# New job orders for all five engines, and two pairs of tensors at another byte offset

## The reference

```python
x = x + _layernorm(_L0_attn_ref(_layernorm(x, axis=-1), w_qkv, b_qkv, w_out, b_out), axis=-1)
x = x + _layernorm(_L0_ffn_ref(_layernorm(x, axis=-1), W1, b1, W2, b2), axis=-1)
```

## Time and profile before

| | |
|---|---|
| median of 3 runs | 2037.46 us (2028.71 to 2041.54) |
| the profiled execution | 2037.54 us, of which the span from first to last instruction is 2035.8 us |
| granted TensorE clock, mean over the span | 0.979 |
| busy: PE, DVE, ACT, POOL | 1906.9, 1496.3, 1416.3, 744.5 us |

### The profile page before, as it was taken

One profiled execution on the slowest core, in us unless ns is written; L12 is line 12 of the kernel. 1 busy time (PEld: TensorE's weight loads), 2 busy tenths in 40 slices (PEclk: granted clock), 3 DMA queues, 4 the chain that ended last, 5 costly groups with the idle time before them and its releaser, 6 DMA issues. The chain is left out here.

```text
span 2035.8 us, 69000 instructions
## 1 busy us (share of the span) xinstructions
PE 1906.9 (94%) x26496; PEld 1547.0 (76%) x26496; DVE 1496.3 (74%) x2690; ACT 1416.3 (70%) x2375; POOL 744.5 (37%) x910
## 2 busy tenths in 40 slices
PE   6779999999999999999999999999999999999975
PEld 5558877778877777878777787777788777777765
DVE  4587887777777877787787778777777887786631
ACT  1556777777767867777777777677777777776653
POOL 2123334344323434333343433333443334333343
PEclk8889999999999999999999999999999999999998
DMA  5454554545545445555544455454455555444320
GB/s 139 94 113 118 121 120 107 125 109 125 121 115 127 107 116 116 121 122 121 124 110 116 116 121 123 120 128 102 114 122 120 122 121 127 107 115 102 81 65 16
DMA packets 203973, 229.65 MB, mean 113 GB/s; under 512 B 67808, under 2 KB 120800, under 8 KB 203744
## 3 DMA queue, kind: packets, MB, share of 16 engines
q1 hardware_dynamic: 201712, 223.36, 46.5%
q10 hardware_dynamic: 2032, 2.69, 0.4%
HBM read 71.77 MB, written 52.43 MB: 61 GB/s over the span
## 5 line engine op out<-in xcount | busy, mean ns | idle before, releaser
L894 DVE TENSOR_REDUCE max_bias<-p_pair 128x4 f32<-128x1024 f32 (+1 forms) x640 | 767.2, 1219 | 293.8 <-PE p_pair L635 171.4
L812 ACT ACTIVATE probs<-p_pair 128x1024 f32<-128x1024 f32 x640 | 642.9, 1031 | 295.5 <-PE p_pair L635 221.8
L1037 POOL TENSOR_TENSOR h_lo<-h_f,h_hi 128x512 fp32r<-128x512 f32 x256 | 338.7, 1324 | 589.7 <-ACT h_hi L849 582.1
L638 PE MATMUL p_pair<-stacks 49*128 49x256 f32 (+1 forms) x3072 | 294.8, 297 | 51.3 <-DVE max_bias L894 20.0
L638 PEld LDWEIGHTS p_pair<-stacks 49*128 49x128 f32 (+1 forms) x3072 | 225.7, 187 | 128.8 <-DVE max_bias L894 40.9
L665 PE MATMUL p_pair<-x_hi,w_hi 64*128 64x256 f32 (+1 forms) x2560 | 303.9, 313 | 4.2 <-DVE x_lo L908 3.8
L665 PE MATMUL p_pair<-w_hi,h_hi 64*128 64x256 f32 x2048 | 291.2, 280 | 12.4 <-POOL h_lo L1037 12.1
L665 PE MATMUL p_pair<-w_lo,h_hi 64*128 64x256 f32 x2048 | 288.7, 277 | 0.0
L665 PE MATMUL p_pair<-w_hi,h_lo 64*128 64x256 f32 x2048 | 288.5, 277 | 0.0
L665 PE MATMUL p_pair<-x_lo,w_hi 64*128 64x256 f32 (+1 forms) x2560 | 287.7, 300 | 0.0
L665 PE MATMUL p_pair<-x_hi,w_lo 64*128 64x256 f32 (+1 forms) x2560 | 287.4, 300 | 0.0
(11 more groups left out here) (80 smaller groups left out, 2706.5 us busy)
## 6 DMA issues: line engine op xcount, KB each, us to landing
stacks<-qk SPq DMA_DIRECT2D x1536, 64.0 KB, 2.3
o_rows<-o_t SPq DMA_DIRECT2D x128, 256.0 KB, 2.2
xr<-x SPq DMA_DIRECT2D x32, 512.0 KB, 6.0
inv_b<-inv_rows SPq DMA_DIRECT2D x64, 256.0 KB, 3.4
ya<-o_rows SPq DMA_DIRECT2D x64, 256.0 KB, 3.5
out<-yf SPq DMA_DIRECT2D x64, 256.0 KB, 2.3
xa<-x SPq DMA_DIRECT2D x31, 512.0 KB, 4.2
shift_rows<-max_t SPq DMA_DIRECT2D x128, 8.0 KB, 2.7
```

Of the source, the lines that this page charges most:

```text
L638: last = nc.tensor.matmul(dst[:, j, col:col + HALF].rearrange("p (a n) -> p a n", a=2), stack[r, stationary, at, kb * P:(kb + 1) * P], two ...
L812: nc.scalar.activation(probs[:, prob_slot(quad, c), :, :], banks("scores", n)[:, :, :], ACT.Exp, scale=SCALE).then_inc(exp_done, 1)
L894: nc.vector.tensor_reduce(dst, src, axis=AX.X, op=ALU.max, negate=True).then_inc(red_done, 1)
L1037: nc.gpsimd.tensor_tensor(h_parts[1][:, m:m + 2, :], h_f[:, n % 2, :, :], h_parts[0][:, m:m + 2, :].bitcast(F32), ALU.subtract).then_inc(h ...
```

## The change

All lists in `ORDER`, `FIRST` and `LAST` are new; the jobs are the same, 70 on PE, 64 on DVE, 46 on ACT, 20 on POOL and 30 on SP in a turn, each once, with some batch offsets and PSUM pairs changed. `FIRST` and `LAST` hold the same work but for where the turns are cut (PE 173 jobs ahead of the loop before, 171 after). No job's instructions change. In SBUF, the four `bn` tensors (96 bytes each, 384 together) move from behind `zeros` to ahead of `o2_t`. So `o2_*`, `h_hi`, `h_lo`, `max_bias`, `max_t`, `values` and the constants start 384 bytes higher, which takes the first five from 64 to 192 modulo 256; `xr` and `x2_*` move by whole multiples of 256. The diff, cut to PE's turn, two lines of DVE's, the start of PE's `FIRST` and the layout:

```diff
 ORDER = {
     "PE": [
-        ("f1", 7, -4, 3), ("scores_max", 1, -1, 2), ("qk", 3, -1, 1), ("scores_max", 2, -1, 0),
-        ("pv", 1, -2, 2), ("scores", 12, -2, 1), ("scores_max", 3, -1, 3), ("f2", 2, -4, 0),
-        ("scores", 13, -2, 2), ("scores_max", 4, -1, 1), ("scores", 14, -2, 3), ("f2", 3, -4, 0),
-        ("max_t", 0, -1, 2), ("scores", 15, -2, 1), ("scores", 16, -2, 3), ("scores_max", 5, -1, 0),
-        ("pv", 2, -2, 2), ("scores_max", 6, -1, 3), ("scores", 17, -2, 0), ("scores_max", 7, -1, 2),
-        ("scores", 18, -2, 1), ("scores_max", 8, -1, 3), ("scores", 19, -2, 0), ("scores_max", 9, -1, 1),
-        ("v", 0, -1, 2), ("scores_max", 10, -1, 3), ("pv", 3, -2, 0), ("x2", 0, -3, 1), ("scores", 0, -1, 3),
-        ("max_t", 1, -1, 0), ("v", 1, -1, 2), ("scores", 1, -1, 0), ("scores", 2, -1, 3), ("f1", 0, -3, 1),
-        ("scores_max", 11, -1, 0), ("x1", 0, 0, 3), ("f1", 2, -3, 2), ("scores", 3, -1, 0), ("f1", 1, -3, 1),
-        ("scores_max", 12, -1, 3), ("qk", 0, 0, 0), ("scores_max", 13, -1, 3), ("f1", 3, -3, 2),
-        ("qk", 1, 0, 0), ("scores_max", 14, -1, 3), ("op", 0, -2, 1), ("max_t", 2, -1, 3), ("op", 1, -2, 1),
-        ("scores", 4, -1, 2), ("f2", 0, -3, 0), ("scores_max", 15, -1, 3), ("scores_max", 16, -1, 2),
-        ("scores", 5, -1, 1), ("f2", 1, -3, 0), ("scores_max", 17, -1, 3), ("scores", 6, -1, 1),
-        ("pv", 0, -1, 2), ("scores", 7, -1, 0), ("scores_max", 18, -1, 1), ("scores", 8, -1, 3),
-        ("f1", 4, -3, 2), ("scores_max", 19, -1, 0), ("scores", 9, -1, 1), ("f1", 6, -3, 3),
-        ("scores", 10, -1, 0), ("scores_max", 0, 0, 1), ("f1", 5, -3, 2), ("max_t", 3, -1, 0), ("qk", 2, 0, 1),
-        ("scores", 11, -1, 0),
+        ("f1", 7, -4, 3), ("scores", 11, -2, 0), ("qk", 2, -1, 1), ("scores_max", 1, -1, 2), ("qk", 3, -1, 1),
+        ("scores_max", 2, -1, 0), ("pv", 1, -2, 2), ("scores_max", 3, -1, 0), ("scores", 12, -2, 1),
+        ("scores_max", 4, -1, 2), ("f2", 2, -4, 3), ("max_t", 0, -1, 0), ("scores", 13, -2, 2),
+        ("scores_max", 5, -1, 1), ("scores", 14, -2, 0), ("f2", 3, -4, 3), ("scores", 15, -2, 2),
+        ("scores_max", 6, -1, 1), ("scores", 16, -2, 0), ("pv", 2, -2, 3), ("scores", 17, -2, 0),
+        ("scores_max", 7, -1, 2), ("scores", 18, -2, 1), ("scores", 19, -2, 3), ("scores_max", 8, -1, 0),
+        ("v", 0, -1, 2), ("scores_max", 9, -1, 1), ("scores", 0, -1, 3), ("pv", 3, -2, 0), ("scores", 1, -1, 1),
+        ("scores_max", 10, -1, 3), ("x2", 0, -3, 0), ("scores", 2, -1, 1), ("v", 1, -1, 2), ("x1", 0, 0, 3),
+        ("max_t", 1, -1, 0), ("f1", 0, -3, 1), ("f1", 2, -3, 2), ("scores_max", 11, -1, 3),
+        ("scores", 3, -1, 0), ("f1", 1, -3, 1), ("scores_max", 12, -1, 3), ("qk", 0, 0, 0),
+        ("scores_max", 13, -1, 3), ("f1", 3, -3, 2), ("scores", 4, -1, 1), ("qk", 1, 0, 0),
+        ("scores_max", 14, -1, 3), ("op", 0, -2, 1), ("max_t", 2, -1, 3), ("op", 1, -2, 1),
+        ("scores", 5, -1, 0), ("f2", 0, -3, 3), ("scores_max", 15, -1, 2), ("scores_max", 16, -1, 1),
+        ("f2", 1, -3, 3), ("scores", 6, -1, 0), ("pv", 0, -1, 2), ("scores", 7, -1, 0),
+        ("scores_max", 17, -1, 1), ("scores", 8, -1, 3), ("f1", 4, -3, 2), ("scores", 9, -1, 0),
+        ("scores_max", 18, -1, 1), ("f1", 6, -3, 3), ("scores", 10, -1, 0), ("scores_max", 19, -1, 1),
+        ("f1", 5, -3, 2), ("scores_max", 0, 0, 0), ("max_t", 3, -1, 1),
     ],
...
     "DVE": [
...
-        ("copy_max", 2, -2), ("qk_lo", 1, -1), ("op_out", 0, -3), ("reduce", 15, -2), ("reduce", 16, -2),
-        ("lny_stats", 0, -3), ("lny_stats", 1, -3), ("f2_out", 0, -4), ("reduce", 17, -2), ("lnf_stats", 0, -4),
...
+        ("op_out", 0, -3), ("reduce", 15, -2), ("f2_out", 0, -4), ("lny_stats", 0, -3), ("reduce", 16, -2),
+        ("lny_stats", 1, -3), ("reduce", 17, -2), ("ln1_mean", 0, 0), ("lny_mean", 0, -3), ("reduce", 18, -2),
...
 FIRST = {
     "PE": [
-        ("x1", 0, 0), ("qk", 0, 0), ("qk", 1, 0), ("scores_max", 0, 0), ("qk", 2, 0), ("scores_max", 1, 0),
-        ("scores_max", 2, 0), ("scores_max", 3, 0), ("qk", 3, 0), ("scores_max", 4, 0), ("scores_max", 5, 0),
-        ("max_t", 0, 0), ("scores_max", 6, 0), ("scores_max", 7, 0), ("scores_max", 8, 0), ("scores_max", 9, 0),
...
+        ("x1", 0, 0), ("qk", 0, 0), ("qk", 1, 0), ("qk", 2, 0), ("qk", 3, 0), ("scores_max", 0, 0),
+        ("scores_max", 1, 0), ("scores_max", 2, 0), ("scores_max", 3, 0), ("scores_max", 4, 0), ("max_t", 0, 0),
+        ("scores_max", 5, 0), ("scores_max", 6, 0), ("scores_max", 7, 0), ("scores_max", 8, 0), ("v", 0, 0),
...
@@ -387,9 +406,11 @@
         xa = sb("xa", [P, KB, D])
         x1_t = [sb(f"x1_{n}", [P, KD, L], F32R) for n in ("hi", "lo")]
         o_t = sb("o_t", [P, 2, L])
-        o2_t = [sb(f"o2_{n}", [P, KD, L], F32R) for n in ("hi", "lo")]
         xr = sb("xr", [P, KB, D])
         x2_t = [sb(f"x2_{n}", [P, KD, L], F32R) for n in ("hi", "lo")]
+        KINDS = ("ln1", "lny", "ln2", "lnf")
+        bn = {n: sb(f"bn_{n}", [P, KB, 6]) for n in KINDS}
+        o2_t = [sb(f"o2_{n}", [P, KD, L], F32R) for n in ("hi", "lo")]
         h_parts = [sb(f"h_{n}", [P, KF, HALF], F32R) for n in ("hi", "lo")]
 
         max_bias = sb("max_bias", [P, 2, 8 * KB + D])
@@ -400,8 +421,6 @@
         values = sb("values", [P, KB, H * VW + 32 - VW])
         minus_half, eps = sb("minus_half", [P, KB]), sb("eps", [P, KB])
         zeros = sb("zeros", [P, P])
-        KINDS = ("ln1", "lny", "ln2", "lnf")
-        bn = {n: sb(f"bn_{n}", [P, KB, 6]) for n in KINDS}
         mv = {n: sb(f"mv_{n}", [P, KB, 2]) for n in KINDS}
         ve = {n: sb(f"ve_{n}", [P, KB]) for n in KINDS}
         rstd = {n: sb(f"rstd_{n}", [P, KB]) for n in KINDS}
```

438 lines of the change are left out of this document (225 added, 213 removed), and 17 rows, old and new, of tables (FIRST, LAST).

## The result

The changed kernel takes 2051.36 us (median of 6, 2048.24 to 2052.92), where the kernel before took 2039.5 (2028.71 to 2046.52) beside it: ratio 1.0066, interval 1.0048 to 1.0085. It is slower by 0.7%; the forecast was 2009 us and its range ended at 2038. The profiled execution took 2052.92 us.

What follows compares the result with a forecast made beforehand. PE, busy 94% of the span, was taken to bound the kernel through matmul pitch, short waits and ramps. Orders 11, layout 13 and start 5 us sum to 29, so 2037.5 becomes 2008.5, say 2009 us; range 1997 to 2018, 8-in-10 1993 to 2038.

Steps and rivals of the forecast that it cites:

- The orders in a turn: Steady-state loop: new orders leave PE's PSUM pair openers 2.38 us short instead of 2.86; taken as 0.4 us a turn, 11 us.
- POOL's list: POOL's new order in the turn: priced at nothing, since POOL is 37% busy and the other distances have room.
- The list of openers: PE's jobs in a turn that come too soon for their pair's reader: seven before, eight after the change.
- R3: Rival, DVE's queue blocks at f2_out 0 ahead of reduce 16: slower, 2050 us at 1 us a turn; chance 0.10.
- Against it: Counter-evidence to R3, on DVE: long o2_lo (1.66 us) are the exception and stand some 8 us ahead of f2_out.
- The layout: PE's f2 and op matmuls: new addresses bring a pair from 0.1177 to 0.1138 us, 13 us in all.
- `f1` job 6: Sign against the layout term: same placement as f1 job 5, yet 0.1175 us a pair, so placement isn't all.
- stream above: Weak sign for the layout term: 512 columns take 443 ns with the stream above its stationary operand, 419 below.
- The start: Batch 0: qk 2 and 3 fill the 7.37 us stack wait, reduce 4 ends near 33 us; gain 5 us.
- The end: Last batch's chain with f2 1 ahead of f1 4 and 6: no gain, plus or minus 3 us.
- R2: Rival, in a turn: removed waits come back at other pairs, orders gain nothing; 2019 or 2032 us, chance 0.19 together.

Runs made afterwards that it cites:

- e1: The changed kernel with the bn tensors back behind zeros (new orders, old layout): 2052.68 us, ratio 1.0079 to the kernel before.
- e7: e3 in the layout of before: 2036.26 us, ratio 1.0001 to the kernel before.
- e15: The changed kernel with POOL's order as in e5, no zero matmuls ahead of scores_max, and the old layout: 2029.52 us, ratio 0.995 to the kernel before.
- e9: The kernel before with the new start alone (qk 2 and 3 of batch 0 ahead of scores_max 0): 2030.82 us, ratio 0.997.
- e3: The changed kernel with lnf_shift 0 behind reduce 5 on DVE and lnf_apply 0 behind exp 14 on ACT: 2032.62 us, ratio 0.9977 to before.
- e5: The changed kernel with POOL alone reordered (lnf_rstd 0 ahead of h_lo 7, ln1_rstd 0 behind both x1_add): 2028.63 us, ratio 0.9968 to before.
- e11: e5 with lnf_shift 1 ahead of reduce 7 on DVE and lnf_apply 1 ahead of exp 19 on ACT: 2044.49 us, ratio 1.0031 to before.

## Why the prediction was wrong

**The sum of the shortfalls.** Between the forecast of 2008.5 us and the profiled 2052.9 lie 44 us: 25 in the 25 turns from batch 3 to batch 28, 10 in the start (of which up to 4.5 are how executions vary) and 10 behind batch 28, each rounded.

**The orders in a turn.** The step that failed is the one that priced the orders by the room between PE's jobs against the length of their readers (2.86 down to 2.38 us, taken as 0.4 a turn), and POOL's list at nothing. It put each reader's start at the moment when PE has done its part. `f2_out` 1 did not start then: its queue was late, by the 1.21 us of `lnf_shift` 0 where it took 0.13 before, and by the wait for its scale. The prediction even had this pair, "`pv` 2 after `f2` 3 (0.72 for 0.83, 0.11)", and the wait was 0.77. I had looked at which DVE jobs stand behind which, but priced POOL's list at nothing because of its 37% busy share. POOL's order matters here not by its load but by what it runs at the moment when a DVE instruction is released. The missing term is 0.6 us a turn in the old layout (e1 against e7, 59.66 to 59.10) and 0.8 in the new, a loss.

The 0.4 us itself isn't borne out either. With the block gone, in the old layout, the turn is 59.10 us (e7, e15) against 59.38 and 59.32 before (before, e9), 0.2 to 0.3 less. But PE's idle time is as long: 39.9 and 38.3 us of the 1440 in e7 and e15, 38.8 and 36.7 in before and e9. So the orders saved no idle time, the gain comes from elsewhere (where is open), and that it lies near 0.4 is luck. The list of openers did poorly too. Of the eight that it had short after the change only `pv` 2, `scores_max` 8 and `x2` wait 0.05 us or more in the mean; `v` 0 (0.65 short) and `scores` 2 (0.44) don't. `x2` waits for `ln2_apply` and not for a reader of its pair, and `max_t` 1 was not on the list.

**R3** was this mechanism in the wrong place. It named a collision of DVE and POOL that delays DVE's queue, a price of 1 us a turn, and 2050 us as the time; the time was 2051. That the two agree is luck, since its sum had the layout at nothing and the start kept. And it set it at `f2_out` 0 and expected waits of `scores_max` 17 and 18, and there are none: DVE idles 1.79 us at `f2_out` 0 in the mean of the turns, and nothing is late behind it. Its 0.10 was too low. "Against it" I counted that long `o2_lo` are the exception. What should have been asked of the new lists is which DVE job waits for POOL and what POOL runs next: `lnf_shift` 0 waits for `lnf_rstd` 0 and `x1_add` 1 follows it, which the diff shows.

**The layout** was right in size on the orders of before: 0.1135 us a pair and 12.9 us, forecast 0.1138 and 13. On the changed orders it gave 1.3 us with the block, which is inside the noise, and 4 to 6 without. As a mechanism it holds in part: the addresses move most jobs from one pitch to the other, not all. `f1` job 6, which the prediction counted against it, was the sign of this. One sign that I took for it was none. The earlier trace rows have 443 ns for `scores_max` and 419 for `scores` at 512 columns, "stream above" and "below". In the changed kernel, where `stacks` lies as it did, the groups read

```profile
L654 PE MATMUL p_pair<-stacks 49*128 49x512 f32 x512 | 112.7, 435 | 3.4 <-ACT probs L831 1.4 <-DMA stacks<-shift_rows 0.9 <-DVE qk L934 0.6
L654 PE MATMUL p_pair<-stacks 48*128 48x512 f32 x512 | 103.8, 410 | 5.9 <-DMA stacks<-qk 4.2 <-ACT probs L831 1.4
```

the other way round. So the addresses of `stacks` alone don't set these means.

**The start** was right as far as it was looked at: `reduce` 4 ends at 34.0 (forecast near 33), and the two moves alone gain 6.3 us (forecast 5). The step that failed is that it ended there. By `reduce` 9 the gain is gone (49.3, before 48.0): `max_t` 0 ahead of `scores_max` 5 with the zero matmuls behind both, and `v` 0 ahead of `scores_max` 9, stand between.

**The end** was priced at nothing, plus or minus 3. It is 5 to 10 us longer, a cost that I did not work out. The traces place it around the last output projection, and the runs have not explained it.

R2 ("a wait removed from one pair comes back at another") is right about the room: without the block PE is idle as long as before. It doesn't explain the loss: e3 and e5 removed the largest wait and got it back.

## What to carry to other kernels

Before a new order is priced, list for each engine the instruction that is released by POOL and the one that POOL starts right behind the release: here a DVE instruction of two columns with two SBUF operands lasted as long as POOL's next one (1.2 us), and everything in DVE's queue shifted by it. A count of room between jobs leaves such delays out, and where it is right the wait may still only move: check a claimed saving against the idle time that is left. Compare a new order at an equal layout, and a layout at equal orders. Split a change with many parts into its parts: here the layout gained 13 us alone, the early `qk` jobs 6, and the other new orders took more than both.

## What the hardware showed that I had not expected

- A two-column DVE instruction took 1.23 us beside a POOL addition of 1.29, and 0.15 alone; and in e11 a `TENSOR_SCALAR` of 256 columns on one SBUF tensor was held up in the same way (1.68 us for two where 0.73 is usual).
- A pair of `f2` matmuls takes about 0.1135 or 0.1178 us, with identical code inside the job and little in between. On the orders of before the addresses decide it for all 100 jobs (stationary operand at 192 or 64 modulo 256 bytes, stream at 128); on the new orders 28 of 100 jobs are slow with the better addresses.
- Zero matmuls ahead of a waiting product raised the granted clock of the start little (0.82 against 0.77 from 40 to 100 us), and cost about 5 us.
